# Value products joined back to back, small products at new places, and the attention's first work made in the stage ahead of it

## What is computed

```python
# layer 0: graph attention
h = _gat(x, adj, W1, a1, W1.shape[1])      # softmax over axis 1 of leaky_relu(Wh1 + Wh2^T), masked by adj > 0, times Wh
h = _gat(h, adj, W2, a2, W2.shape[1])
h = _layernorm(x + h, g_ln1, b_ln1)
src = _layernorm(h + relu(h @ w_ff1 + b_ff1) @ w_ff2 + b_ff2, g_ln2, b_ln2)
# layer 1: relational attention, 8 heads of 16
attn = softmax(q k^T / 4)
out = sum over r in 0..3 of (attn * (adj == r)) @ v_r
x = _ln(src + out @ Wo + bo, g1, beta1)
y = _ln(x + gelu(x @ W1 + b1) @ W2 + b2, g2, beta2)
```

## Time and profile before

| | |
|---|---|
| median of 3 runs | 1249.26 us |
| profiled execution, and its span | 1250.93 us, 1249.1 us |
| busy: TensorE | 1092.9 us (87%) |
| VectorE | 962.1 us (77%) |
| ScalarE | 742.4 us (59%) |
| GpSimd | 614.3 us (49%) |
| chain that ended last, share of TensorE | 10%, all of it in the third stage |
| last work of the first stage, last scores of the second | 446.93 us, 1090.96 us |
| costliest groups | GpSimd L1387 473.4 us; VectorE L1251 343.6; ScalarE L1116 262.0; the two of TensorE's L1042 136.4 and 136.3 |

### The profile page before, as it was taken

The page is one execution under the profiler, slowest core; times in us unless marked ns, Lnnn a source line. Parts: engine busy times, 40 slices in busy tenths (PEclk is TensorE's granted clock), DMA queues, the critical chain, the costliest instruction groups (busy, mean ns, idle before and its releaser), DMA issues. The chain is left out here.

```text
span 1249.1 us, 21656 instructions
## 1 busy us (share of the span) xinstructions
PE 1092.9 (87%) x6087; PEld 501.8 (40%) x6087; DVE 962.1 (77%) x2313; ACT 742.4 (59%) x1341; POOL 614.3 (49%) x515
## 2 busy tenths in 40 slices
PE   4588888888888549999999999999999999979996
PEld 3465665665664312233332333323333233234443
DVE  2878878878877537788888888888888888618777
ACT  3477677677675323666666666666666666644442
POOL 3311311311300135878887788878888787900000
PEclk9799999999998857999999999999999999979998
DMA  5222112112100242321333213332133320000000
GB/s 168 92 76 77 50 63 88 50 54 97 50 1 1 86 118 70 106 66 50 111 110 97 69 53 109 110 93 70 57 109 110 89 73 8 2 0 34 34 34 34
DMA packets 49413, 86.50 MB, mean 69 GB/s; under 512 B 8787, under 2 KB 35795, under 8 KB 44246
## 3 DMA queue, kind: packets, MB, share of 16 engines
q1 hardware_dynamic: 46454, 85.56, 22.3%
q10 hardware_dynamic: 2912, 0.40, 0.2%
HBM read 52.12 MB, written 29.36 MB: 65 GB/s over the span
## 5 line engine op out<-in xcount | busy, mean ns | idle before, releaser
L1387 POOL TENSOR_TENSOR b_picked<-b_prob,b_mask 128x512 f32<-128x512 f32 x384 | 473.4, 1260 | 129.8 <-ACT b_prob L1116 129.7
L1251 DVE TENSOR_REDUCE b_top<-b_peak 128x1 f32<-128x512 f32 x512 | 343.6, 687 | 87.7 <-PE b_peak L1003 82.6
L1116 ACT ACTIVATE b_prob<-b_score 128x1024 f32<-128x1024 f32 x256 | 262.0, 1023 | 193.3 <-PE b_score L1018 191.5
L812 POOL TENSOR_TENSOR a_hw_n<-a_hw,a_inv 128x512 f32<-128x512 f32 x16 | 19.5, 1219 | 274.2 <-DVE a_inv L700 261.1
L1042 PE MATMUL b_o_ps<-b_picked,b_dval 128*32 128x512 f32 x1024 | 136.4, 604 | 12.7 <-DVE b_picked L1265 10.2
L1042 PE MATMUL b_o_ps<-b_prob,b_val 128*32 128x512 f32 x1024 | 136.3, 604 | 0.3 <-ACT b_o_t L1127 0.3
L1265 DVE TENSOR_TENSOR b_picked<-b_prob,b_mask 128x512 f32<-128x512 f32 x128 | 113.0, 883 | 1.5 <-ACT b_prob L1116 1.4
L1003 PE MATMUL b_peak<-shared 96*128 96x512 bf16 x256 | 103.4, 409 | 3.6 <-DVE b_top L1251 3.5
L645 ACT ACTIVATE a_att<-a_att,a_least 128x512 f32<-128x512 f32 x128 | 91.1, 716 | 17.3 <-DVE a_least L673 16.8
L1003 PE MATMUL b_peak<-b_k_stack,b_q_stack 96*128 96x512 bf16 x256 | 98.3, 384 | 0.0
L673 DVE CUSTOM_DVE_ANT_0 a_att<-a_att,a_no_edge 128x512 f32<-128x512 f32 x128 | 97.2, 778 | 0.0
(11 more groups left out here) (176 smaller groups left out, 1807.6 us busy)
## 6 DMA issues: line engine op xcount, KB each, us to landing
a_adj_in<-in_adj SPq DMA_DIRECT2D x16, 1024.0 KB, 5.4
scratch<-shared SPq DMA_DIRECT2D x32, 384.0 KB, 2.6
shared<-scratch SPq DMA_DIRECT2D x16, 768.0 KB, 6.8
scratch<-shared SPq DMA_DIRECT2D x32, 256.0 KB, 2.6
b_q_stack<-scratch SPq DMA_DIRECT2D x8, 768.0 KB, 5.5
b_k_stack<-scratch SPq DMA_DIRECT2D x8, 768.0 KB, 8.0
a_x_in<-in_x SPq DMA_DIRECT2D x16, 256.0 KB, 2.7
xs<-in_x SPq DMA_DIRECT2D x16, 256.0 KB, 5.5
```

The source lines that it names most:

```text
L1116: act.activation(prob[s % 2][:, 2 * u:2 * u + 2, :], score[u][:, :, :], ACT.Exp, scale=float(DH) ** -0.5).then_inc(sem("exp_ready"), 1)
L1251: dve.tensor_reduce(top[g][:, hh, c:c + 1], peak[hh % 2][:, :], AX.X, ALU.max, negate=True).then_inc(sem("peak_read"), 1)
L1387: pool.tensor_tensor(picked[(NR * s + rel) % 2][:, hh, :], prob[s % 2][:, hh, :], m, ALU.mult).then_inc(sem("picked_pool"), 1)
```

## The change

**1. The step on TensorE.** `weigh_picked` is put directly ahead of `weigh(None)`, and the picked products now are those of two steps back (s-2), the unmasked ones still those of one step back. Where s % 4 == 1 the group of `o_ps` ends, and `weigh_picked` stands alone at the step's begin. ITEMS has new places: o1 goes from step 3 to 1, k from 1 to 3, the top items from early to mid, turn_o from 4 early to 3 mid, v0 and v1 from late in 2 and 6 to early in 4 and 6. ScalarE copies `o_ps` first in a step.

**2. The step on VectorE.** For s > 0 the mid item now stands ahead of the reduction of peak 3, before it stood behind it.

**3. The first stage's tail**, t = 16 to 18, is written out (`tail`). In it are q and k of batches 0 and 1 with their splits and stores, the stack loads, the values and masks of batch 0, 24 peaks of batch 0 and their reductions over three banks, the first top item, and the flag with its turning. The prologue turn b = -1 is gone. Rows of ones come by DMA and no longer by GpSimd's memsets.

**4. `see`** is one OR of 512 words per step of the first stage, and `between()` runs ahead of leak 3.

```diff
         ITEMS = {
-            0: [(0, "mid", "q", 2), (1, "mid", "k", 2), (2, "early", "top1", 0), (2, "late", "v0", 1), (3, "mid", "o1", -1),
-                (4, "early", "turn_o", -1), (4, "mid", "out", -1), (5, "mid", "y", -1), (6, "early", "top0", 1),
-                (6, "late", "v1", 1), (7, "mid", "o0", 0)],
+            0: [(0, "mid", "q", 2), (1, "mid", "o1", -1), (2, "mid", "top1", 0), (3, "early", "k", 2),
+                (3, "mid", "turn_o", -1), (4, "early", "v0", 1), (4, "mid", "out", -1), (5, "mid", "y", -1),
+                (6, "early", "v1", 1), (6, "mid", "top0", 1), (7, "mid", "o0", 0)],
...
-            for b in range(-1, 2):
-                turn(b, b % 2)
+            for b in range(2):
+                turn(b, b)
...
-                    b, par, s = moved(t, par, s, -1)
+                    b, par, s = moved(t, par, s, -1 if rel is None else -2)
...
                     for s in range(S):
+                        ends = s % C == 1
+                        if ends:
+                            weigh_picked(b, par, s)
                         peaks(b, par, s, 0)
                         scores(b, par, s, 0)
                         for name, by in items(path, s, "early"):
                             item(b, name, by)
                         peaks(b, par, s, 1)
+                        if not ends:
+                            weigh_picked(b, par, s)
                         weigh(b, par, s, None)
                         peaks(b, par, s, 2)
                         scores(b, par, s, 1)
                         for name, by in items(path, s, "mid"):
                             item(b, name, by)
                         peaks(b, par, s, 3)
-                        for rel in range(NR):
-                            weigh(b, par, s, rel)
-                        for name, by in items(path, s, "late"):
-                            item(b, name, by)
...
                         peaks(b, par, s, 2)
+                        if s > 0:
+                            for name, by in items(path, s, "mid"):
+                                item(b, name, by)
                         peaks(b, par, s, 3)
-                        for name, by in items(path, s, "mid"):
-                            item(b, name, by)
+                        if s == 0:
+                            for name, by in items(path, s, "mid"):
+                                item(b, name, by)
...
+            def see(b):
+                words = codes[:, b, :, :].rearrange("p c n -> p (c n)").bitcast(I32)
+                first = isinstance(b, int) and b == 0
+                if not first:
+                    dve.wait_ge(codes_seen, b)
+                dve.tensor_tensor(seen[:, :], words if first else seen[:, :], words, ALU.bitwise_or).then_inc(codes_seen, 1)
...
                 for c in chunks:
                     if c + 1 < C:
+                        if c == 2:
+                            between()
                         leak(k, b, c + 1, s2)
-                    if c == 2 and k == 0:
-                        between()
                     mask(k, b, c)
...
                 if first:
                     invert(0, t - 1)
                     scale_rows(t - 1)
+                    see(t - 1)
```

The last step of the tail on TensorE and on VectorE, where `peaks` and `most` are the maxima of batch 0:

```diff
+                turn_h(B - 1)
+                peaks(3, 5)
+                turn_n(B - 2)
+                for f in range(FC):
+                    feed_up(B - 1, f)
+                    peaks(5 + 2 * f, 7 + 2 * f)
+                feed_down(B - 1, (13, 15, 16, 16, 16))
+                pe.wait_ge(sem_b("values0_kept"), 2)
+                first_qk.turn_top(pe, row[0])
+                peaks(16, 18)
+                turn_y(B - 1)
+                peaks(18, 20)
+                pe.wait_ge(other_made, 1)
+                pe.transpose(pair[0:1, 1, 0:P], other[:, :], ident[:, :]).then_inc(other_turned, 1)
+                turn_n(B - 1)
+                peaks(20, 24)
...
+                most(0, 16)
+                first_qk.split_top(dve, row[0])
+                add_h(B - 1)
+                most(16, 18)
+                norm_stats(1, B - 1)
+                most(18, 20)
+                norm_shift(B - 1)
+                dve.wait_ge(other_turned, 1)
+                dve.tensor_reduce(widest[:, :], pair[0:1, 1, 0:P], AX.X, ALU.max).then_inc(flag_step, 1)
+                dve.wait_ge(flag_step, 1)
+                dve.tensor_scalar(general[:, :], widest[:, :], 0.5, None, ALU.is_gt).then_inc(flagged, 1)
+                most(20, 24)
```

More of the change, by code:

```diff
@@ new lines, in values, with keep_values @@
+    def values(self, pe, bank, half):
+        D, w = self.z.D, self.w
+        for k in range(2):
+            c = 2 * half + k
+            at = bank[:, 2 * k * D:2 * (k + 1) * D]
+            pe.matmul(at, w["ones"][:, :], w["bias3"][:, 0:2 * D], start=True, stop=False)
+            mm = pe.matmul(at, self.x_own[:, c * P:(c + 1) * P], w["wv"][:, 0:2, :].rearrange("p r d -> p (r d)"),
+                           start=False, stop=True)
+        mm.then_inc(self.sem("values0_done"), 1)
+    def keep_values(self, act, bank, half):
+        D, DH = self.z.D, self.z.DH
+        act.wait_ge(self.sem("values0_done"), half + 1)
+        for k in range(2):
+            c = 2 * half + k
+            src = bank[:, 2 * k * D:2 * (k + 1) * D].rearrange("p (r h d) -> p r h d", r=2, h=HEADS)
+            act.copy(self.val0[:, c, :, 0:DH], src[:, 0, :, :])
+            last = act.copy(self.dval0[:, c, :, 0:DH], src[:, 1, :, :])
+        last.then_inc(self.sem("values0_kept"), 1)
@@ new lines, in mask, with peak @@
+    def mask(self, act, half):
+        chunks = slice(2 * half, 2 * half + 2)
+        act.copy(self.mask0[:, chunks, :], self.codes[:, 0, chunks, :])
+    def peak(self, pe, banks, n):
+        R6, g, s, hh = 6 * self.z.DH, n // 16, n // 4, n % 4
+        h, c = 4 * g + hh, s % 4
+        if n == 0:
+            pe.wait_ge(self.sem("stacked"), 32)
+        if n >= len(banks):
+            pe.wait_ge(self.sem("peak_read"), n - len(banks) + 1)
+        pe.matmul(banks[n % len(banks)], self.q_stack0[0:R6, h, c * P:(c + 1) * P], self.k_stack0[0:R6, h, :],
+                  start=True, stop=True).then_inc(self.sem("peak_ready"), 1)
@@ L371, in steps @@
                 step(t, True, True, True, True, True)
[L372 to L373 removed]
+            step(B - 1, True, True, True, True, False)
         def encode(eng, b, chunks):
@@ L529, in step @@
                     feed_up(t - 3, 3)
-                if last:
-                    first_qk.product(pe, bank0, 1)
-                if feed:
                     feed_down(t - 3)
                 if second:
-                    if not begin:
-                        pe.wait_ge(summed[0], t - 2)
                     round_two(t - 2)
@@ new lines, in keep_h, with keep_hw @@
+            def keep_h(b):
+                act.wait_ge(h_turned, b + 1)
+                act.wait_ge(mid_done, FC * b)
+                act.wait_ge(summed[1], b)
+                act.activation(h_t[:, :], out[:, :], ACT.Identity, bias=w["col"]["L0_gnn_b_ln1"],
+                               scale=w["col"]["L0_gnn_g_ln1"]).then_inc(h_t_ready, 1)
+            def keep_hw(b):
+                act.wait_ge(hw_done, b + 1)
+                if not (isinstance(b, int) and b == 0):
+                    act.wait_ge(scaled[1], b)
+                act.copy(hw[:, :, :].rearrange("p (a c) d -> p a (c d)", a=2),
+                         pair[:, :, 0:2 * (D + 2)]).then_inc(hw_ready, 1)
@@ L909, in count @@
             def count(turn, end):
-                return sum(0 <= t + by < end for t in range(-2, turn + 1)
+                return sum(0 <= t + by < end for t in range(turn + 1)
                            for n, (_, _, _, by) in enumerate(ITEMS[path]) if t < turn or n < pos)
```

478 lines of the change are left out of this document (307 added, 171 removed).

## The result

The changed kernel takes 1212.53 us (median of four runs, 1210.64 to 1213.58), the kernel before 1249.02 (four runs). The ratio is 0.9705 with a 95% interval of 0.9689 to 0.9722, so it is 36.5 us faster. The forecast was 1226, with a range from 1207 to 1243: right in direction, inside the range, and 13.5 us too slow.

What follows compares the result with a forecast made beforehand. TensorE was taken to bound the attention turns, a dependency chain the stretch ahead of them. Terms -28.1 - 4.6 - 5.2 + 1.5 - 20.2 - 9.9 + 43.5 = -23.0 us gave 1227.9 profiled, 1226 for the median, range 1207 to 1243.

Steps and rivals of the forecast that it cites:

- A, the handover: Last x kept to first scores: 33.26 us falls to about 5.2, as queries, keys and maxima move into the tail; -28.1.
- B, the tail: First stage's tail: OR chain gone -9.2, reductions +2.6, TensorE's peaks +2.0; sum -4.6 us.
- C, the loop: First-stage steps: earlier reciprocal gives back 0.4 us each, OR covered by the wait for a_low; -5.2 over 13 steps.
- D, the clock: Around the handover: turns starting at half clock +4 us, faster clock in the first stage's last steps -2.5; sum +1.5.
- E, the turns: Attention turns: joined value products -20.2 us, no wait for the pick -9.9, new waits +43.5; period about 40.
- a join: In the turns, two adjacent groups of value products: each saves 0.21 us, six in each of 16 turns, -20.2.
- the wait for the pick: In the turns, TensorE no longer waits for VectorE's pick, as picked products come a step later; -9.9 us.
- the new waits: In the turns, peaks wait for reductions on two banks, chiefly behind o0 and o1; 2.9 us a turn, +43.5.
- (a): Rival for the turns: reductions keep ahead, no new waits; 1183 us, or up to 1205; chance 0.10.
- (c): Rival for the turns: two banks are too few, waits 5.4 us a turn, 37 more, 1263 us; chance 0.05.
- (d): Rival for the turns: joined value products save nothing, +20, 1246 us; chance 0.05.
- (b): Rival for the first stage: the OR is on the path, each step grows by 0.69 us, 1240; chance 0.08.

Runs made afterwards that it cites:

- e8: Changed kernel with the last four peaks of the first stage's tail ahead of the last batch's transposes: 1208.65 us.
- e3: Changed kernel with round two's reciprocal again behind the last leak of round one: 1225.12 us.
- e2: Changed kernel with ScalarE copying hw again behind the two small functions of round two's norm: 1218.37 us.
- e4: Changed kernel with a second OR of 512 words on VectorE in each first-stage step: 1215.88 us.
- e10: Changed kernel with the edits of e1, e2 and e3 together, the OR of each step kept: 1239.42 us.
- e1: Changed kernel with GpSimd's encoding waiting again for round one's last mask, not for the OR: 1225.45 us.
- e6: Changed kernel with all of VectorE's small items again behind the step's fourth reduction: 1201.52 us.
- e7: Changed kernel with the six joins of a turn undone, picked products ahead of the step's second peak: 1218.42 us.
- e9: Changed kernel with e8's edit and only step 2's small item ahead of VectorE's fourth reduction: 1192.06 us.
- e12: e9 with the six joins of a turn undone as in e7: 1215.22 us.

## Why the prediction was right, and where it was off

**A, the handover.** Right in kind and 2.4 us too large. The stretch without work that the prediction had at 4.97 us stayed (425.79 - 420.76 = 5.0). But it begins only when the last reductions are through, 420.76 us, 2.1 after the last x: their peaks stand behind transposes that waited 4.20 us for ScalarE. I had put all 24 maxima inside the tail. With these peaks ahead (e8) the last x is followed by the first scores after 5.36 us, not 7.56. Whether the 5.0 us are the branch's, or belong to GpSimd's memsets (421.05 to 423.00) and the loads issued behind them (423.76 to 426.05), no run tried.

**B, the tail.** -10.7 where B and its part of D gave -7.1. The OR chain's wait went. The two terms that come in were both too large. For the reductions between the sum a_y_t and the last x (+2.6) the rows give +0.4: from the one to the other it is 7.33 us (410.52 to 417.85) where it was 6.97 (439.18 to 446.15). They stand where VectorE had waited 1.21 us for the transposes and 0.60 for the next small function, and the transposes take 0.66 us where they took 1.12. For TensorE's peaks (+2.0) the stretch from the last but one x to that sum is 10.78 us where it was 21.63; with 9.2 of it for the OR chain this is -1.7. I had priced a peak at 0.53 us, at half clock; in the last step the granted clock is 0.93, and two peaks in a row there start 0.22 us apart. How much of the difference is the clock's and how much the new order's was not tried.

```profile
399.74 0.78 ACT L815 ACTIVATE xs<-a_mid,columns 128x512 f32<-128x512 f32 x1
410.52 0.73 DVE L1033 SCALAR_TENSOR_TENSOR a_y_t<-a_out,columns,a_h_t 128x512 f32<-128x512 f32 x1
411.30 0.66 PE L513 MATMUL a_mid<-ident,a_y_t 128*128 128x128 f32 x4 [0.91 <-DVE a_y_t L1033]
```

**C, the loop.** This step of the prediction failed: "-0.4 a step" measured -1.28, beyond even the end of -0.86 that it had been given. That the total stayed inside the range is owed to the range's width of 17 to 19 us. Three things were missed.
- I priced the earlier reciprocal by VectorE's collision alone, of which only 0.23 us came back (1.29 where it was 1.52), since 0.75 us of the multiplication still lie over the mask and not 0.45. It starts GpSimd 0.8 us sooner, and TensorE was waiting for just that (25.3 us in 16 steps before, 11.4 after). e3 puts it at 1.09 us.
- I left out ScalarE's earlier copy of hw, though the diff shows it: 0.58 (e2).
- I costed the OR at nothing by the wait for a_low. The cover was right in the end and the named cover wrong. It stands in the wait for TensorE's transposes (e4). Without the other three edits it costs 0.66 (e10), where the rows have it at 1.61 us beside the encoding, too long for the 0.90 us that VectorE waits there. The encoding's wait, which starts it later, I had not priced at all; without it the loop loses 1.20 (e1).

The single edits undone add 2.87 us, more than the 1.94 from 24.30 to 22.36, so they aren't independent.

The Trainium skill, "GPSIMD Engine Reference", specification table, names two cases in which VectorE contends with GpSimd: an instruction with two SBUF inputs, and one in a 2-port mode. The mask has two SBUF inputs, and the trace agrees: beside GpSimd's multiplication (277.42 to 278.46 us) it takes 1.29 us, against 0.68 alone. For the leak, with one input in PSUM, the trace doesn't contradict the rule, but it is no test: only its last 0.4 us lie beside the multiplication, and in the kernel before a mask whose last 0.3 us lay beside it (290.17 to 290.83, the multiplication from 290.52) took 0.66 us and wasn't slowed either.

```profile
277.08 0.72 DVE L863 SCALAR_TENSOR_TENSOR a_att<-a_row,a_s_own,a_low 128x512 f32<-128x512 f32 x1
277.71 1.29 DVE L870 CUSTOM_DVE_ANT_0 a_att<-a_att,a_no_edge 128x512 f32<-128x512 f32 x1
```

The scalings have one SBUF tensor input and did contend, 2.64 against 0.88 us. That would be the rule's other case; no run here shows in which mode they ran.

**D, the clock.** Too large. Behind the first scores TensorE is at half clock for 6.0 us (426.19 to 432.2), where it was 3.8: 2.2 more, and I had taken 8 more. Half of that is 1.1 us where I had +4. The table agrees: with 12.5 of the +14.3 in the 15 periods, at most 1.8 are left for this. Its other part, the higher clock in the tail (-2.5), stands with B.

**E, the turns.** Right, term by term: a join 0.21 to 0.23 us (0.21), the wait for the pick gone, the new waits 2.8 us a turn by the timeline (2.9), the period 39.97 (about 40). The lost time stands where I put it, behind o0 (0.76), o1 (0.70), and in what follows. VectorE's order as the cause of most of them is shown by e6. What a join pays in the period is less plain: taking out all six costs 0.34 us a turn in the changed kernel (e7), and 1.69 where VectorE's order is e9's (e12), both with the wait of turn_o in it. So joins pay more once the waits are small; that they pay their full 1.4 is not shown.

**The rivals.** (a) and (c) fell with the waits at 2.8 us a turn. (d) fell with the pair's 2.17 us. (b) did not hold for the new loop. In the old one its 0.69 us a step would have come out (0.66), but from an OR slowed to 1.61 us.

## What to carry to other kernels

Price an edit that moves an instruction by what it lets start elsewhere, first of all the engine whose wait on it has a row. Where an edit adds a wait to a third engine, ask what that engine did beside whom. When transitions are saved on the bound engine, look at what the removed instructions between had covered: here six joins worth 1.4 us a turn by their distances made a difference of 0.34 to the period until a second engine's order was set to them, and then of 1.69, a wait of 0.7 that comes with undoing them included.

## What was not expected of the hardware

- GpSimd's encoding (int32 in, bf16 out) slowed VectorE's scalar multiplications from 0.88 to 2.64 us for four, in e1, and to 1.76 in the kernel before, though it ran beside all of them in both. It slowed the OR from 0.68 to 1.61 us in e10, but not in e1, where the OR also began beside it (295.15 us, the encoding from 291.60 to 296.80). What decides this no run shows.
- TensorE's clock in the tail: with 20 more peaks and further products ahead of its end, the granted clock was 1.00, 1.00 and 0.93 in the last three steps, where it was 0.93, 0.87 and 0.68 before. The work moved into the gaps came with a faster clock for the work around it; that the one caused the other was not tried.
